# Attention division moved under the tail, output by chunks, shorter roots, one table load and two orders moved, in an eight-stage transformer kernel

## The chip, the core and the metric

The kernel runs on one core of one Trainium2 chip. The core has TensorE (PE in the profile, with PEld for its weight loads), VectorE (DVE), ScalarE (ACT), GpSimd (POOL) and SyncE, whose queue (SPq) issues most transfers. The metric is the device time of one execution in microseconds, lower is better. The time before is the median of three executions, 3603.91 us (3601.78 to 3606.88). The profiled execution took 3613.86 us, with a span of 3612.1 us from its first to its last instruction.

## What is computed

Eight stages follow one another on 4096 tokens of width 128: four times an attention-like layer and a mixture of experts, each behind a layer norm and added to the stream `x`. Only what the change touches is shown.

```python
def _layernorm(x, axis=-1, eps=1e-05):
    m = jnp.mean(x, axis=axis, keepdims=True)
    v = jnp.var(x, axis=axis, keepdims=True)
    return (x - m) / jnp.sqrt(v + eps)
...
# layer 0 and layer 1 attention (16 heads of 8; layer 1 causal)
    probs = jax.nn.softmax(scores, axis=-1)
    a_dot = jnp.einsum('bnst,btnd->bsnd', probs, v4)
...
# layer 0 also reads a memory through elu(q)
    out = (a_dot * (1.0 - w) + a_mem * w).reshape(B, S, D_MODEL)
...
# layer 2 attention: two selective scans, forward and backward
    u = jnp.swapaxes(jax.nn.silu(xc + conv_b[None, :, None]), 1, 2)
...
# layer 3 mixture, the last stage: 16 routed experts and a shared one
    y = jnp.einsum('bsed,bse->bsd', ye, combine).astype(x.dtype)
    x = x + _L3_ffn_ref(_layernorm(x, axis=-1), ...)
```

## The kernel before

`x` and `h` lie in SBUF as [128 features, 4096 tokens] and are worked on in 8 chunks of 512 (`NB`, `chunk(c)`). Each stage is one or more blocks. In a block every engine has its own list of instructions, in the order in which the code writes them, and engines meet through semaphores; a block ends when all its engines are through. No scheduler moves anything: what stands first in the code of an engine is issued first, and an instruction that waits holds up all behind it on that engine.

**Norm.** `layer_norm` (five times), `layer_norm_twice` (once) and the head of `mixture` (four times) take means and variances on TensorE, the square root on ScalarE, and then a chain of small VectorE operations on [128, 32] (a Newton step on the reciprocal root, then a split into three bf16 parts), each waiting for the one before it (`Chain`). TensorE then spreads the root over the chunks.

**First projection.** `layer0_project` runs 8 passes. In pass c ScalarE copies q, k and v out of PSUM with some functions of q, then squares three weight tiles of the next mixture (`sq`, a ring of 3, line 1447), then does `copy_num(c-1)` (line 1411) and `widen(c-1)` (line 1417). TensorE in its pass c does the denominators and numerators of c, the projection of c+2, counts the squares of the pass (`count_squares`, lines 1374 and 1378, forms of one column), and last `spread_inverse(c)` (line 1366), which needs `widen(c)`, that is the end of ScalarE's pass c+1. `sq` of job n needs the count of job n-3.

**Second projection.** `pattention` with `a=a` (names a1q_) does the same for layer 1. SyncE stores for each chunk v, then the three parts of q (ready by VectorE, line 1846), then the three parts of k (ready by GpSimd, line 1694), then issues loads for the attention to come. The chunk buffers are used in turns of two, so ScalarE's copies for chunk c wait for the stores of chunk c-2.

**Attention.** `attend` handles query blocks b of 512 in 8 steps; the products of a block lag half a block behind its scores. The row maxima go out through a small DRAM buffer (line 1040) and come back into the queries (line 1043), both by GpSimd's DMA queue; TensorE's `scores_of_keys` waits for them. Numerators and denominators of each block and group of four heads (`pv_sb`, 256 KB) are stored by SyncE at line 947 in `a.pv`. At the end SyncE waits for all these stores (line 986), and the block ends.

**Division.** `combine` is a block of its own. It loads the 128 rows of denominators (line 1557) and, in four buffers, the numerators of the 8 blocks (line 1561). GpSimd builds 0/1 matrices (`pick`); VectorE inverts the denominators (line 1584); TensorE spreads them over the rows (line 1579); VectorE multiplies (line 1590, or 1592 and 1595 where the result is weighted and added to `x`).

**Scan and end.** In the norm before the scan ScalarE ends with Exp (line 2008), and the scan begins with SiLU (line 2163). The last mixture adds its chunks to `x` (line 715); a block behind it stores `x` in one transfer of 2 MB (line 2968).

## Time and profile before

| | us |
|---|---|
| three executions | 3603.91, 3601.78, 3606.88 |
| the profiled execution | 3613.86 |
| its span | 3612.1 |
| first projection | 32.0 to 137.5 |
| first attention | 137.5 to 552.8 |
| its division | 552.8 to 573.0 |
| first mixture | 573.0 to 1080 |
| second projection | 1104 to 1195.3 |
| second attention | 1195.3 to 1561 |
| its division | 1561 to 1578 |
| rest of layer 1 | 1578 to 1940 |
| scan | 1985.8 to 2940 |
| last mixture | 3180 to 3612.1 |

The mean granted TensorE clock over the span is 0.926 of full speed. The page names the releaser of an idle time behind an arrow: `[1.72 <-ACT ...]` says that the engine was idle for 1.72 us and that ScalarE ended it. In the rows a timeline entry with `x3` is a run of like instructions, whose length is from the start of the first to the end of the last. In the view of stretches the busy times follow in the order PE, PEld, DVE, ACT, POOL, then come the granted clock, the DMA share and GB/s.

### The profile page before, as it was taken

How to read it: one execution, taken by the hardware profiler on the slowest of the kernel's cores; microseconds unless marked ns; L12 is line 12 of the kernel's file. 1: busy time of each engine (PE TensorE's matmuls, PEld its weight loads, DVE VectorE, ACT ScalarE, POOL GpSimd, SP SyncE). 2: the span in 40 equal slices, each digit the busy share in tenths (PEclk: the TensorE clock that was granted, in tenths of full speed). 3: DMA queues.
4: the chain of work that ended last, by engine and by line, in shares of the span. 5: the costliest groups of instructions: out<-in, count | busy, mean ns of one | idle time of the engine just before them, and what ended most of it. 6: DMA issues, size and time to landing. Idle time of an engine off the chain costs nothing. (4 is left out here: it accounts for less than half of the span.)

```text
span 3612.1 us, 39566 instructions
## 1 busy us (share of the span) xinstructions
PE 3240.8 (90%) x12845; PEld 1536.3 (43%) x12845; DVE 2450.0 (68%) x4164; ACT 1820.7 (50%) x2881; POOL 1191.2 (33%) x1010
## 2 busy tenths in 40 slices
PE   8899998999997699979998789898898789889999
PEld 5422224444444354535544233333333354764443
DVE  4788874443338577746544899999999955656544
ACT  5366672444446355534333777777777633312221
POOL 4211110000002222210000799999999910210000
PEclk7699998999998799989899899999999979889999
DMA  4222201000002533110000443443443410000000
GB/s 129 66 69 65 61 31 33 1 0 1 1 19 81 132 88 91 60 39 1 1 1 25 153 153 147 148 157 144 155 152 147 147 45 3 1 1 1 0 1 24
DMA packets 113335, 232.14 MB, mean 64 GB/s; under 512 B 27701, under 2 KB 82378, under 8 KB 95754
## 3 DMA queue, kind: packets, MB, share of 16 engines
q1 hardware_dynamic: 109034, 228.02, 19.0%
q0 software_dynamic: 4096, 1.59, 0.2%
q8 instruction: 104, 1.70, 0.2%
q14 instruction: 101, 0.83, 0.1%
HBM read 191.46 MB, written 34.87 MB: 63 GB/s over the span
## 5 line engine op out<-in xcount | busy, mean ns | idle before, releaser
L1199 DVE TENSOR_REDUCE a_top<-a_sc 128x1 f32<-128x512 f32 (+3 forms) x1024 | 547.2, 584 | 162.3 <-PE a_sc L1075 102.5
L2406 POOL TENSOR_TENSOR a_g<-a_g,a_spread 128x1024 f32<-128x1024 f32 x255 | 597.7, 2363 | 41.4 <-DVE a_g L2336 40.8
L2336 DVE TENSOR_TENSOR_SCAN a_g<-a_decay,a_drive 128x512 f32<-128x512 f32 x510 | 587.1, 1201 | 16.3 <-ACT a_drive L2225 12.9
L1156 ACT ACTIVATE a_prob<-a_st 128x1024 f32<-128x1024 f32 (+2 forms) x512 | 422.5, 862 | 280.7 <-PE a_st L1092 182.9
L705 DVE TENSOR_TENSOR f_s<-f_a,f_spread 128x512 f32<-128x512 f32 x392 | 269.4, 687 | 381.8 <-PE f_y L547 170.6
L2084 PE MATMUL a_y<-a_g,ident 128*128 128x512 f32 x1024 | 481.0, 610 | 31.3 <-POOL a_g L2406 31.3
L538 PE MATMUL f_hid<-h,f_w 128*128 128x512 f32 x784 | 404.2, 597 | 0.0
L547 PE MATMUL f_y<-f_s,f_w 128*128 128x512 f32 x784 | 401.6, 594 | 2.6 <-DVE f_s L705 2.6
L2209 ACT ACTIVATE a_decay<-a_delta,a_capped_a 128x512 f32<-128x512 f32 x512 | 331.8, 710 | 12.4 <-DVE a_g L2336 9.7
L1072 PE MATMUL a_sc<-a_k,a_q 96*128 96x512 bf16 (+3 forms) x1024 | 311.4, 357 | 20.9 <-POOL a_mask_k L996 11.2
L2084 PEld LDWEIGHTS a_y<-a_g,ident 128*128 128x128 f32 x1024 | 198.4, 197 | 306.7 <-issue 246.1
L602 ACT ACTIVATE f_a<-f_hid,f_b,f_norms 128x512 f32<-128x512 f32 x256 | 198.8, 777 | 255.2 <-PE f_hid L538 255.2
L1089 PE MATMUL a_st<-a_q,a_k 128*128 128x512 bf16 (+3 forms) x1024 | 284.0, 346 | 29.9 <-DMA a_q<-a_max_rows 28.2
L1107 PE MATMUL a_pv<-a_prob,a_v 128*32 128x512 f32 (+3 forms) x2048 | 234.7, 527 | 0.6 <-ACT a_prob L1156 0.3
L620 POOL CAST f_gates_f<-f_gates_b 96x512 f32<-96x512 bf16 x24 | 14.7, 612 | 653.6 <-ACT f_gates_b L583 653.6
L547 PEld LDWEIGHTS f_y<-f_s,f_w 128*128 128x128 f32 x784 | 146.4, 189 | 196.4 <-issue 177.5
L2380 POOL TENSOR_TENSOR a_pd<-a_du_s,a_spread 128x1024 f32<-128x1024 f32 x96 | 227.2, 2366 | 0.1
L602 ACT ACTIVATE f_a<-f_hid 128x512 f32<-128x512 f32 x136 | 81.2, 597 | 289.6 <-PE f_hid L535 289.6
L753 DVE TENSOR_TENSOR f_m<-f_a,f_hid 128x512 f32<-128x512 f32 x136 | 93.6, 688 | 181.0 <-ACT f_a L602 180.6
L538 PEld LDWEIGHTS f_hid<-h,f_w 128*128 128x128 f32 x784 | 148.0, 191 | 158.0 <-issue 151.7
L2325 DVE TENSOR_TENSOR a_drive<-a_du,a_spread 128x512 f32<-128x512 f32 x320 | 203.6, 682 | 0.0
L1089 PEld LDWEIGHTS a_st<-a_q,a_k 128*128 128x128 bf16 x1024 | 86.9, 98 | 252.4 <-ACT a_prob L1156 114.6
(396 smaller groups left out, 4903.0 us busy)
## 6 DMA issues: line engine op xcount, KB each, us to landing
a_spread<-a_bc_rows SPq DMA_DIRECT2D x128, 1024.0 KB, 4.6
a_q<-a_q_rows SPq DMA_DIRECT2D x192, 96.0 KB
a_pv_rows<-a_pv_sb SPq DMA_DIRECT2D x48, 256.0 KB, 2.0
a_k<-a_k_rows SPq DMA_DIRECT2D x288, 32.0 KB
a_k<-a_k_rows SPq DMA_DIRECT2D x288, 16.0 KB
a_num<-a_pv_rows SPq DMA_DIRECT2D x16, 256.0 KB, 3.6
a_pv_rows<-a1q_vf SPq DMA_DIRECT2D x16, 256.0 KB, 2.1
a_q_rows<-p_qp SPq DMA_DIRECT2D x24, 128.0 KB
```

What stands on the lines that cost most here:

```text
L538: nc.tensor.matmul(hid[:, n % 4, :], unit.w1, h[:, chunk(c)], start=True, stop=True).then_inc(f.hidden, 1)
L547: nc.tensor.matmul(y[:, :], f.units[u].w2, s[:, (n - LAG) % R, :], start=(u == 0), stop=(u == U - 1 and f.b2 is None)).then_inc(f.used, 1)
L602: nc.scalar.activation(a[:, n % R, :], hid[:, slot, :], f.func, bias=unit.bias if unit.bias is not None else 0.0, scale=unit.scale if unit ...
L705: nc.vector.tensor_tensor(s[:, n % R, :], (m if gated else a)[:, n % R, :], spread[:, k % 2, :], ALU.mult).then_inc(f.scaled, 1)
L1072: last = nc.tensor.matmul(sc[:, at % 3, 0:w], q[k][0:MAX_AT, n, t * P:(t + 1) * P], kk[k][0:MAX_AT, n // HK, 0:w], start=True, stop=not a. ...
L1089: last = nc.tensor.matmul(st[:, j % 2, col:col + wide], kk[k][:, n // HK, key:key + P], q[k][:, n, first:first + wide], start=True, stop=n ...
L1156: nc.scalar.activation(prob[w % 2][:, j, 0:width(kp)], st[:, j % 2, 0:width(kp)], ACT.Exp, scale=a.scale).then_inc(s.exp_done, 1)
L1199: nc.vector.tensor_reduce(top[:, t, n:n + 1], sc[:, slot(4 * n + t) % 3, 0:w], AX.X, ALU.max).then_inc(s.maxed, 1)
L2084: last = nc.tensor.matmul(y[:, k, :], S.ident[:, :], g[:, n % 8, k, :], start=False, stop=(n == STATES - 1))
L2209: last = nc.scalar.activation(decay[:, n % 4, k, :], delta[:, d, k, :], ACT.Exp, scale=capped_a[d][:, k, n:n + 1])
L2336: nc.vector.tensor_tensor_scan(to, decay[:, n % 4, k, way], drive[:, k, way], 0.0, ALU.mult, ALU.add).then_inc(scanned, 1)
L2406: nc.gpsimd.tensor_tensor(g[:, n % 8, :, :], g[:, n % 8, :, :], spread[:, pair % 4, 2 + n % 2:3 + n % 2, :].to_broadcast([P, H2, L]), ALU. ...
```

## The change

Six things are changed. They are shown here cut to their core.

1. **Roots.** In all ten norms the separate addition of EPS goes, and three operations with three operands take the place of four (in `layer_norm_twice`, where the two additions stay, two take the place of three).
2. **Output.** In the last mixture SyncE stores each chunk when it is added; the block behind it is gone.
3. **Table.** ScalarE does a SiLU of one column at the end of the scan's norm.
4. **Division.** Its buffers lie in the query and key buffers of even blocks (`a.q`, `a.k`). When the scores of block 6 are done, SyncE loads the denominators of blocks 0 to 6 (112 rows) and the first four numerators within the attention block, ahead of the last three stores; GpSimd builds the pick matrices and VectorE inverts the 112 rows there. The wait for the last stores moves into the division's block, where the last 16 rows of denominators come as four small transfers and are inverted between chunks 4 and 5.
5. **First projection.** `copy_num(c-1)` and `widen(c-1)` stand ahead of the squares.
6. **Second projection.** The parts of k are stored ahead of those of q.

```diff
-            chain = Chain(dve, S.ln_step, 7 * call)
-            nc.vector.tensor_scalar(v[:, :], var[:, :], EPS, None, ALU.add)
+            chain = Chain(dve, S.ln_step, 6 * call)
             chain(nc.vector.reciprocal(rstd[:, :], std[:, :]))
-            chain(nc.vector.tensor_tensor(v[:, :], v[:, :], rstd[:, :], ALU.mult))
-            chain(nc.vector.tensor_tensor(v[:, :], v[:, :], rstd[:, :], ALU.mult))
-            chain(nc.vector.tensor_scalar(v[:, :], v[:, :], -0.5, 1.5, ALU.mult, ALU.add))
-            chain(nc.vector.tensor_tensor(rstd[:, :], rstd[:, :], v[:, :], ALU.mult))
+            chain(nc.vector.scalar_tensor_tensor(v[:, :], var[:, :], EPS, rstd[:, :], ALU.add, ALU.mult))
+            chain(nc.vector.scalar_tensor_tensor(v[:, :], v[:, :], -0.5, rstd[:, :], ALU.mult, ALU.mult))
+            chain(nc.vector.scalar_tensor_tensor(rstd[:, :], v[:, :], 1.5, rstd[:, :], ALU.add, ALU.mult))
...
-def mixture(nc, S, f):
+def mixture(nc, S, f, out=None):
...
+            if out is not None:
+                for c in range(NB):
+                    sp.wait_ge(f.added, c + 1)
+                    sp.dma_start(out[:, chunk(c)], S.x[:, chunk(c)]).then_inc(S.stored, 16)
+                sp.wait_ge(S.stored, 16 * NB)
...
@@ attend, sync @@
                 body(b, True, True, b % 2)
+            sp.wait_ge(s.st_done, (nB + NB - 1) * 32)
+            for k in range(2):
+                sp.wait_ge(s.pv_stored[k], 16 * 2 * (nB + NB - 1))
+            sp.dma_start(m.den[0:EARLY, :], m.rows[0:EARLY, DH, :]).then_inc(m.den_loaded, 16)
+            for b in range(4):
+                sp.dma_start(m.num[:, b, :], m.rows[H * b:H * b + H, 0:DH, :]).then_inc(m.num_loaded[b], 16)
             body(NB, False, True, 0)
-            for k in range(2):
-                sp.wait_ge(s.pv_stored[k], 16 * 2 * (nB + NB))
+            a.pv_landed = [(s.pv_stored[k], 16 * 2 * (nB + NB)) for k in range(2)]
...
@@ attend, gpsimd and vector @@
+            pool.wait_ge(s.st_done, (nB + NB - 1) * 32)
+            build_picks(nc, pool, m)
...
+            dve.wait_ge(m.den_loaded, 16)
+            nc.vector.reciprocal(m.den[0:EARLY, :], m.den[0:EARLY, :]).then_inc(m.inverse, 1)
...
@@ layer0_project, scalar @@
                 nc.scalar.activation(vf[k][:, :, :], v_ps[:, :, 0:KV], ACT.Copy).then_inc(s.copied, 1)
+                if c >= 1:
+                    copy_num(c - 1)
+                    widen(c - 1)
                 for n in jobs_of(c):
...
-                if c >= 1:
-                    copy_num(c - 1)
-                    widen(c - 1)
...
+EARLY = H * (NB - 1)
+def build_picks(nc, pool, m):
+    nc.gpsimd.memset(m.pick, 0.0).then_inc(m.picked, 1)
+    nc.gpsimd.memset(m.pick_last, 0.0).then_inc(m.picked, 1)
+    nc.gpsimd.memset(m.den_last, 1.0).then_inc(m.picked, 1)
+    pool.wait_ge(m.picked, 3)
...
@@ combine, sync @@
+            for landed, value in a.pv_landed:
+                sp.wait_ge(landed, value)
+            sp.wait_ge(m.picked, 5)
+            for q in range(4):
+                sp.dma_start(m.den_last[32 * q:32 * q + H, :], m.rows[EARLY:EARLY + H, DH, q * P:(q + 1) * P]
+                             ).then_inc(m.last_loaded, 16)
+            for b in range(4, NB):
+                sp.wait_ge(m.multiplied, b - 3)
+                sp.dma_start(m.num[:, b % 4, :], m.rows[H * b:H * b + H, 0:DH, :]).then_inc(m.num_loaded[b % 4], 16)
...
@@ combine, tensor @@
+                if b < NB - 1:
+                    last = nc.tensor.matmul(inv[:, b % 4, :], m.pick[0:EARLY, b, :], m.den[0:EARLY, :],
+                                            start=True, stop=True)
+                else:
+                    pe.wait_ge(m.last_inverse, 1)
+                    for q in range(4):
+                        last = nc.tensor.matmul(inv[:, b % 4, q * P:(q + 1) * P], m.pick_last[:, q, :], m.den_last,
+                                                start=True, stop=True)
...
@@ combine, vector @@
-            dve.wait_ge(den_loaded, 16)
-            nc.vector.reciprocal(den[:, :], den[:, :]).then_inc(inverse, 1)
             for b in range(NB):
+                if b == 5:
+                    dve.wait_ge(m.last_loaded, 64)
+                    nc.vector.reciprocal(m.den_last, m.den_last).then_inc(m.last_inverse, 1)
...
@@ pattention, sync @@
+                    sp.wait_ge(pj.k_parts, pc + c + 3)
+                    store_parts(sp, a.k_rows, c, kp[k], pj.stored[k])
                     sp.wait_ge(pj.q_parts, pc + c + 3)
                     store_parts(sp, a.q_rows, c, qp[k], pj.stored[k])
-                    sp.wait_ge(pj.k_parts, pc + c + 3)
-                    store_parts(sp, a.k_rows, c, kp[k], pj.stored[k])
...
@@ layer2_mamba, Prepare.scalar @@
+                nc.scalar.activation(warm[:, :], S.eps[:, 0:1], ACT.Silu)
```

Three places show how the instructions stand. The first is ScalarE in the first projection, from the copy of k in pass 1 to the copy of q in pass 2. Before:

```order
L1437 ACTIVATE p_k<-p_qk_ps 64x512
L1439 ACTIVATE p_kp<-p_k 64x512
L1441 ACTIVATE p_v<-p_v_ps 128x256
L1447 ACTIVATE p_sq<-f_w 128x512 x3
L1411 ACTIVATE p_num_f<-p_num 128x512
L1417 ACTIVATE p_inv_w<-p_inv_t 128x512
L1424 ACTIVATE p_q<-p_qk_ps 128x512
```

After:

```order
L1446 ACTIVATE p_k<-p_qk_ps 64x512
L1448 ACTIVATE p_kp<-p_k 64x512
L1450 ACTIVATE p_v<-p_v_ps 128x256
L1420 ACTIVATE p_num_f<-p_num 128x512
L1426 ACTIVATE p_inv_w<-p_inv_t 128x512
L1459 ACTIVATE p_sq<-f_w 128x512 x3
L1433 ACTIVATE p_q<-p_qk_ps 128x512
```

The three squares moved behind the copy of the numerators and the widening.

The second is SyncE's queue at the end of the first attention and in its division; the branches are the ends of blocks. Before:

```order
L843 DMA a_q<-a_q_rows 24x4x512
L846 DMA a_k<-a_k_rows 8x2x512 x3
L947 DMA a_pv_rows<-a_pv_sb 128x512 x9
L875 UNCONDITIONAL_BRANCH
L1555 UNCONDITIONAL_BRANCH
L1557 DMA a_den<-a_pv_rows 128x512
L1561 DMA a_num<-a_pv_rows 128x1x512 x8
```

After (the new names `a_q` and `a_k` are the buffers that the denominators and numerators now share with queries and keys):

```order
L842 DMA a_q<-a_q_rows 24x4x512
L845 DMA a_k<-a_k_rows 8x2x512 x3
L947 DMA a_pv_rows<-a_pv_sb 128x512 x6
L987 DMA a_q<-a_pv_rows 112x512
L989 DMA a_q<-a_pv_rows 128x1x512 x4
L947 DMA a_pv_rows<-a_pv_sb 128x512 x3
L875 UNCONDITIONAL_BRANCH
L1591 UNCONDITIONAL_BRANCH
L1597 DMA a_k<-a_pv_rows 16x128 x4
L1601 DMA a_q<-a_pv_rows 128x1x512 x4
```

Five loads moved ahead of the last three stores, and four small ones are new.

The third is ScalarE from the scan's norm into the scan. Before:

```order
L2008 ACT_TABLE_LOAD
L2008 ACTIVATE a_neg_a<-a_pack 128x32 x2
L122 UNCONDITIONAL_BRANCH
L2453 UNCONDITIONAL_BRANCH
L2163 ACT_TABLE_LOAD
L2163 ACTIVATE a_u<-a_bank,a_pack 128x512 x2
```

After:

```order
L2048 ACT_TABLE_LOAD
L2048 ACTIVATE a_neg_a<-a_pack 128x32 x2
L2049 ACT_TABLE_LOAD
L2049 ACTIVATE a_warm<-eps 128x1
L122 UNCONDITIONAL_BRANCH
L2494 UNCONDITIONAL_BRANCH
L2204 ACTIVATE a_u<-a_bank,a_pack 128x512 x2
```

The load of the SiLU table moved from the scan's block into the norm's, with one small operation behind it.

## Rows read from the trace of the kernel before

**Rows 1.** The page, section 1: engine, busy us, share of span, instructions.
```profile
PE 3240.8 (90%) x12845; PEld 1536.3 (43%) x12845; DVE 2450.0 (68%) x4164; ACT 1820.7 (50%) x2881; POOL 1191.2 (33%) x1010
```

**Rows 2.** The timeline at the end (start us, us, engine line op).
```profile
3605.41 0.34 SPq L2968 DMA_DIRECT2D out_xT<-x  x1
```

**Rows 3.** The DMA issues by line: queue, count, KB each, median us to landing.
```profile
a_pv_rows<-a_pv_sb SPq DMA_DIRECT2D x48, 256.0 KB, 2.0
...
out_xT<-x SPq DMA_DIRECT2D x1, 2048.0 KB, 6.3
```

**Rows 4.** The timeline, VectorE, first norm's root, and one three-operand operation.
```profile
23.28 0.19 DVE L193 TENSOR_SCALAR ln_v<-ln_var 128x32 f32<-128x32 f32 x1 [3.99 <-ACT ln_std L232]
...
24.66 0.18 DVE L200 CAST ln_parts<-ln_rstd 128x32 bf16<-128x32 f32 x1
...
1996.98 0.19 DVE L2287 SCALAR_TENSOR_TENSOR a_capped_a<-a_bank,a_neg_a 128x32 f32<-128x32 f32 x1
```

**Rows 5.** The timeline, ScalarE, where the scan begins.
```profile
1985.84 1.28 ACT L2163 ACT_TABLE_LOAD   x1 [14.13 <-PEq L122]
...
1987.14 1.27 ACT L2163 ACTIVATE a_u<-a_bank,a_pack 128x512 f32<-128x512 f32 x2
```

**Rows 6.** The timeline around the end of the first attention and its division.
```profile
534.62 15.57 SPq L947 DMA_DIRECT2D a_pv_rows<-a_pv_sb  x3
...
552.84 0.32 SPq L1557 DMA_DIRECT2D a_den<-a_pv_rows  x1
...
555.58 3.35 DVE L1584 RECIPROCAL a_den<-a_den 128x512 f32<-128x512 f32 x1 [22.56 <-DMA a_den<-a_pv_rows]
...
561.23 0.69 DVE L1592 TENSOR_TENSOR a_num<-a_num,a_inv 128x512 f32<-128x512 f32 x1 [2.30 <-PE a_inv L1579]
...
571.97 0.75 DVE L1595 SCALAR_TENSOR_TENSOR x<-a_num,w_dot,x 128x512 f32<-128x512 f32 x1
```

**Rows 7.** The stretches, same place: PE, PEld, DVE, ACT, POOL busy, then PEclk.
```profile
551.00:552.00 1.00, 0.00 (x0) 0.00 (x0) 0.00 (x0) 0.00 (x0) 0.00 (x0) 1.00 0.42 154
```

**Rows 8.** The timeline at the end of the second attention and its division.
```profile
1558.68 0.32 SPq L947 DMA_DIRECT2D a_pv_rows<-a1q_vf  x1
...
1569.69 0.69 DVE L1590 TENSOR_TENSOR a_g<-a_num,a_inv 128x512 f32<-128x512 f32 x1 [2.30 <-PE a_inv L1579]
...
1577.11 0.69 DVE L1590 TENSOR_TENSOR a_g<-a_num,a_inv 128x512 f32<-128x512 f32 x1 [0.16 <-DMA a_num<-a_pv_rows]
```

**Rows 9.** The DMA issues between 1545 and 1580 us.
```profile
a_num<-a_pv_rows SPq DMA_DIRECT2D x8, 256.0 KB, 3.8
```

**Rows 10.** The timeline, TensorE waiting for a DMA, quiet and beside block loads.
```profile
538.05 0.11 PEld L1089 LDWEIGHTS a_st<-a_q,a_k 128*128 128x128 bf16 x2 [0.88 <-DMA a_q<-a_max_rows]
...
1237.17 0.10 PEld L1089 LDWEIGHTS a_st<-a_q,a_k 128*128 128x128 bf16 x1 [8.35 <-DMA a_q<-a_max_rows]
```

**Rows 11.** The view of line 1043, a_q<-a_max_rows, its last line.
```profile
DMA to landing us min/median/max: 2.0/2.3/6.3
```

**Rows 12.** The timeline, TensorE in the first projection's loop.
```profile
73.69 2.07 PE L1366 MATMUL p_spread<-ident,p_inv_w 128*128 128x128 f32 x8 [1.72 <-ACT p_inv_w L1417]
...
82.39 1.04 PE L1345 MATMUL p_v_ps<-p_wkv,h 128*128 128x64 f32 x8
...
87.83 2.08 PE L1366 MATMUL p_spread<-ident,p_inv_w 128*128 128x128 f32 x8 [1.72 <-ACT p_inv_w L1417]
```

**Rows 13.** The timeline, ScalarE in that loop.
```profile
84.30 0.63 ACT L1447 ACTIVATE p_sq<-f_w 128x512 f32<-128x512 f32 x1 [5.82 <-PE p_sums L1374]
```

**Rows 14.** The stretches in that loop, columns as in rows 7.
```profile
113.00:114.00 1.00, 1.00 (x8) 1.00 (x7) 0.00 (x0) 1.00 (x3) 0.00 (x0) 0.58 0.18 52
```

**Rows 15.** The timeline, SyncE and GpSimd in the second projection.
```profile
1129.00 1.21 POOL L1694 TENSOR_TENSOR a1q_kp<-a1q_k_rest,a1q_kp 128x512 bf16<-128x512 f32 x1
...
1133.13 1.87 SPq L1224 DMA_DIRECT2D a_q_rows<-a1q_qp  x3
```

**Rows 16.** The timeline, ScalarE, last chunk of the second projection.
```profile
1185.57 0.60 ACT L1780 ACTIVATE a1q_qp<-a1q_q_ps 128x512 bf16<-128x512 f32 x1 [2.79 <-DMA a_k_rows<-a1q_kp]
```

115 lines of the change are left out of this document (54 added, 61 removed).

## The prediction

> **What bounds the kernel now.** I read the engine totals first. TensorE is busy for 3240.8 us, 90% of the span [rows 1], so a change pays only where TensorE also stands still, or where a serial tail has no TensorE work in it. I then read the timeline at the joints which the diff touches. At each, the reader should ask which instruction ends last and who is free meanwhile. The profiled execution took 3613.86 us against a median of 3603.91, which is 0.28% more. I work out differences in it and carry them over as they are, since none is a share of the whole.
>
> **Output.** The last instruction of the program is one store of 2 MB [rows 2]; stores of its kind land 6.3 us after issue, one of 256 KB after 2.0 us [rows 3]. By chunks, seven of eight stores lie beside the last chunks' work, and only the last one's landing is left: 6.3 - 2.0 = **-4.3 us**. If the joint with the removed block costs something too, it is a few tenths more. If the stores still queued up, it could not exceed the old landing, so the bounds are 0 and -4.5.
>
> **Roots.** From the first VectorE step of the root to the split into parts, 24.66 - 23.28 = 1.38 us pass, in six waits of one step for the next, some 0.23 us each [rows 4]. A three-operand operation of the same size takes 0.19 us there, as the two-operand one does, so the fused steps are not longer. Of the chain before the split stand the division, a little longer than the rest (0.38), and three steps of 0.225: 1.05 us. That is 0.32 us in nine norms and 0.25 in the tenth: **-3.1 us**. TensorE waits for the root in each, so nothing hides it; the bounds are -2 and -4.
>
> **Table.** When the scan begins ScalarE has been idle for 14.13 us; it loads its table for 1.28 us and starts the SiLU 1.30 us after the load began [rows 5]. The load moves into that idle time: **-1.3 us**. What it costs if the 14.13 us were not there is the same 1.3 us, earlier. The row shows 0.02 us between load and SiLU. The Trainium skill (page "ScalarE: Activation LUTs", section "What ACT_TABLE_LOAD costs") gives about 1283 ns for the load, which the trace agrees with (1.28 us), and about 1380 ns of draining besides, which the trace doesn't show. By that page the term would be -2.7 and the sum 1.4 us lower.
>
> **Division of the first attention.** Its last store is issued by 534.62 + 15.57 = 550.19 us. Then, one after the other, the stores land, the denominators are loaded (issued 552.84), VectorE inverts them from 555.58 for 3.35 us, and the first product starts at 561.23, 2.30 us behind the inverse; the last ends at 572.72 [rows 6]. In the new order the block ends when the last store is issued. With some 0.3 us for the joint, TensorE starts the first spread at 550.5, with its inverse done. It comes straight from work: the stretch behind 551 shows the full clock (1.00) [rows 7]. So I take 1.1 us for the first spread and its wait; the old 2.30 bounds it from above. First product 551.6. The products' chain of 572.72 - 561.23 = 11.49 us stays, 1.44 a block. The second inversion is of 128 columns and adds 3.35 x 128/512 = 0.84, with its wait 0.9. Last product ends at 551.6 + 11.49 + 0.9 = 564.0: -8.7 us. Numerators 4 to 7 must be there: the last stores land by 550.2 + 2.0 = 552.2, four small loads go out by 553.5, numerator 4 follows and lands 3.8 us later [rows 9], at about 557.9, and product 4 is due at 551.6 + 4 x 1.44 = 557.4. So this is just in time; at most 0.5 us is lost.
>
> Against it stands what moves ahead. 1.25 MB of loads are now issued near 535 to 537.5 us, ahead of the last three stores on SyncE's queue, and the last block's queries wait there for their row maxima: TensorE already stood for 0.88 us at 538.05, and where block loads ran beside that round trip it stood for 8.35 us [rows 10]. The landing of that load is 2.0, 2.3 or 6.3 us (minimum, median, maximum) [rows 11]. So the early loads cost from 0 to 6.3 - 2.2 = 4.1 us. No row has five large loads in just this place; I take +1.5, nearer the quiet end, since the denominators' load is spread over 112 rows and the round trip is half over when they go out. Net **-7.2 us** (-4.6 to -8.7).
>
> **Division of the second attention.** Last store issued by 1559.0, first product 1569.69, last ends 1577.80 [rows 8]. New: first product at 1559.0 + 0.35 + 1.1 = 1560.4. Here a block takes only 8.11/8 = 1.01 us, so the transfers come last: stores land 1561.0, four small loads until 1562.2, numerator 4 issued then and landing 0.6 + 3.8 us later at 1566.6, while its product would be due at 1564.5. From there product 4, the second inversion (0.9) and three products of 0.69 end at 1570.2: -7.6. The same contention, with less traffic around, is +0.7 (0 to 4): **-6.9 us**.
>
> **First projection.** TensorE's passes are 87.83 - 73.69 = 14.14 us apart, and each begins with 1.72 us of waiting for the widened inverse of ScalarE, which stands behind the three squares [rows 12]. There are four such waits. The squares themselves wait for the counts (5.82 us) [rows 13], so ScalarE is not the bound but sits in a ring with TensorE: counts at a pass's end let the squares run, these let the widening run. With the widening ahead of the squares, the spread no longer waits for it: 3 x 1.72, and 1.2 for the first, where ScalarE now has to wait some 0.5 us for VectorE's inverse before it gets to its squares: **-6.4 us**. The bounds are 0, if a wait of the counts for the squares takes the old one's place, and more by what a better clock gives (a rival below).
>
> **Second projection.** GpSimd has the parts of k ready at 1129.00 + 1.21 = 1130.2, SyncE issues the store of q's at 1133.13 for 1.87 us [rows 15] and only then k's. The row of k's store first lets its 1.9 us of issuing begin before q's are there. The last chunk's ScalarE copy waits 2.79 us for that buffer's store [rows 16]; of it the PSUM copy's own readiness leaves about 0.8. **-2.0 us** (0 to -2.8). Other chunks don't gain: TensorE sets their pace.
>
> **Sum:** -4.3 - 3.1 - 1.3 - 7.2 - 6.9 - 6.4 - 2.0 = -31.2, so the forecast is 3603.9 - 31.2 = **3572.7 us** (the profiled execution's span would become about 3581). No step is expected to cost time elsewhere: the pick matrices are built by GpSimd in blocks where it has nothing else left.
>
> **Rivals.**
>
> *The clock stays up in the first projection.* Between 73.69 and 82.39 us, 8.7 us, TensorE runs at 1.2 GHz [rows 12], and forms that take half as long at 2.4 GHz could save up to 4.35 us a pass. ScalarE's own work would then bound the pass at about 10.2 instead of 12.4 us, so 2.2 us over four or five passes: 9 to 11 us more, 3562. For it: the waits of 1.72 us, idle time ahead of the slow part, vanish. Against it: the granted clock was at 0.58 between 113 and 114 us with TensorE busy for the whole of that stretch, in the counting of one column a form [rows 14]; it fell without idleness. The Trainium skill (page "TensorE: Matmul & The Clock Gate", section "Part 1: The HAM clock gate") ties the half clock to an idle engine; by that rule this rival would be the forecast; the row speaks against it. Chance 0.13.
>
> *Contention at both tails is large.* Each round trip of the last row maxima takes 6.3 us, not 2.3: 4.1 - 1.5 + 4 - 0.7 = 6 us worse, 3578.5. For it: the 8.35 us wait [rows 10]; against it: the large loads go out while the round trip is partly done. Chance 0.2.
>
> *One large part does not do what it says.* Either the ring of squares holds the passes at 14.14 us, so that the wait turns up ahead of the counts, or an attention's early block end is lost because the last products or copies of the block end later than the last store's issue by some microseconds. Either costs 6 to 7 us; both give 3585. Chance 0.13 that one or both hold.
>
> *Slower.* The buffers of the division are those of the even query blocks. If the layout or the shifted loads disturb the second attention at its block ends, the row maxima of every block could meet block loads as at 1237.17. One such wait costs 8.35 - 0.88 = 7.5 us; seven of them make 52 us, for a total of 3625. It decides from about five such new waits, where the gain of 31 us is used up. Against it: within blocks 0 to 6 the order of SyncE's queue is the same as before, only the tail moves. Chance 0.02.
>
> **How the numbers follow.** The forecast has a chance of 0.52, between 3566 and 3578: its bounds are the single terms' (first spread up to 1.1 us later in either division, contention 2 us either way, projection 3 us). I reach up to 3585 for the two rivals above it and down to 3560 for the clock, which leaves out less than 2 in 10. Faster by over 0.2%, about what a measurement of this kernel can tell from no change, means below 3596.7, and all but the slower rival and a coincidence of failures lie there: 0.94. Within 0.2%: 0.04; slower: 0.02.
>
> **What would show it.** In the changed trace: a last store of 256 KB, landing in about 2 us; some 1.05 us from the root's first step to its split; no table load in the scan's block; a first product within 1.5 us of each attention's last issued store, a small inversion of about 0.85 us, last products near 13 and 11 us behind that store; TensorE's wait for the last row maxima under 3 us (about 6 if the second rival holds); passes of 12.4 us without a wait ahead of the spread (10 with the clock high, 14 if the ring holds); the last chunk's ScalarE wait near 0.8 us. Wrong would be: new waits at the row maxima of earlier blocks, a wait for squares ahead of the counts, or numerators 4 to 7 landing late by more than 2 us.

## The result

The changed kernel took 3559.88 us in the median of four executions (3552.98 to 3563.64), the kernel before, measured beside it, 3605.39 us (3601.78 to 3614.10). The ratio is 0.9868, with a 95% interval of 0.9844 to 0.9892: about 47 us less, where 31 were forecast. The measured median lies 0.12 us below the range's low end of 3560. In a second comparison the changed kernel had 0.9874 (0.9853 to 0.9896).

The two profiled executions differ by more: spans of 3612.1 and 3557.1 us, 55 us. To see where, I use marks that both traces have, and the time between each mark and the next. "Cast" is VectorE's rounding of the row maxima, of which each attention has 32. "First inverse" is VectorE's first reciprocal of the projection's denominators (`p_inv_t`).

| stretch (us) | before | after | difference | forecast |
|---|---|---|---|---|
| first projection, from its first inverse to the first cast | 104.95 | 88.27 | -16.7 | -6.4 |
| first attention, first to last cast | 380.48 | 380.26 | -0.2 | 0 |
| last cast to last product of its division | 40.37 | 31.29 | -9.1 | -7.2 |
| double norm and second projection, to the first cast | 118.12 | 115.37 | -2.8 | -2.3 |
| second attention, first to last cast | 336.27 | 325.36 | -10.9 | 0 |
| last cast to last product of its division | 33.88 | 25.65 | -8.2 | -6.9 |
| start of the last addition to the end of the span | 7.65 | 3.08 | -4.6 | -4.3 |

The engine totals after, beside [rows 1]: TensorE is still busy for 90% of a shorter span.

```profile
PE 3212.4 (90%) x12785; PEld 1527.4 (43%) x12857; DVE 2441.6 (69%) x4147; ACT 1820.5 (51%) x2882; POOL 1193.7 (34%) x1016
```

The end, from the timeline of VectorE and SyncE and the list of transfers after 3540 us, answers to [rows 2, 3]: the last chunk is added at 3554.02, its store is issued 0.02 us after that and lands in 2.0 us.

```profile
3554.02 0.69 DVE L716 TENSOR_TENSOR x<-x,f_y 128x512 f32<-128x512 f32 x1 [1.48 <-PE f_y L548]
...
3554.73 0.33 SPq L459 DMA_DIRECT2D out_xT<-x  x1
```

```profile
out_xT<-x SPq DMA_DIRECT2D x1, 256.0 KB, 2.0
```

The root in the first norm, beside [rows 4]: 24.36 - 23.29 = 1.07 us where it was 1.38, with each fused operation at the 0.19 us of a plain one.

```profile
23.29 0.35 DVE L193 RECIPROCAL ln_rstd<-ln_std 128x32 f32<-128x32 f32 x1 [3.98 <-ACT ln_std L230]
23.68 0.19 DVE L194 SCALAR_TENSOR_TENSOR ln_v<-ln_var,ln_rstd 128x32 f32<-128x32 f32 x1
23.91 0.19 DVE L195 SCALAR_TENSOR_TENSOR ln_v<-ln_v,ln_rstd 128x32 f32<-128x32 f32 x1
24.13 0.19 DVE L196 SCALAR_TENSOR_TENSOR ln_rstd<-ln_v,ln_rstd 128x32 f32<-128x32 f32 x1
24.36 0.18 DVE L198 CAST ln_parts<-ln_rstd 128x32 bf16<-128x32 f32 x1
```

ScalarE at the scan's start, beside [rows 5]: the second table load now stands behind the first one's work, and the SiLU starts without one. What was 15.4 us from the Exp's end to the SiLU is 14.3 us here (12.9 in the second trace of the changed kernel). The 1.4 us between the two traces are the clock's, as far as the rows show: TensorE ends this wait, and its granted clock over the stretch was 0.68 here and 0.76 there (0.70 before).

```profile
1923.38 1.28 ACT L2049 ACT_TABLE_LOAD   x1
1924.67 0.20 ACT L2049 ACTIVATE a_warm<-eps 128x1 f32<-128x1 f32 x1
1937.65 1.26 ACT L2204 ACTIVATE a_u<-a_bank,a_pack 128x512 f32<-128x512 f32 x2 [12.78 <-PEq L122]
```

The first division, beside [rows 6]. These lines are of SyncE and VectorE, in order of time. The early loads go out at 507.64 to 510.78, the inversion of 112 rows (3.33 us) stands inside the attention, the last store is issued by 532.67, the first product starts 1.8 us behind it, and the last ends 13.8 us behind it (22.5 before).

```profile
507.64 0.34 SPq L987 DMA_DIRECT2D a_q<-a_pv_rows  x1
508.03 2.75 SPq L989 DMA_DIRECT2D a_q<-a_pv_rows  x4
...
515.15 0.68 DVE L1196 CAST a_max_row<-a_sc 16x512 bf16<-16x512 f32 x1 [2.52 <-PE a_sc L1127]
515.76 3.33 DVE L1216 RECIPROCAL a_q<-a_q 112x512 f32<-112x512 f32 x1
...
525.97 6.70 SPq L947 DMA_DIRECT2D a_pv_rows<-a_pv_sb  x2
...
534.47 0.69 DVE L1632 TENSOR_TENSOR a_q<-a_q,a_inv 128x512 f32<-128x512 f32 x1 [15.38 <-PE a_inv L1611]
...
541.39 0.95 DVE L1625 RECIPROCAL a_k<-a_k 128x128 f32<-128x128 f32 x1
...
545.69 0.75 DVE L1635 SCALAR_TENSOR_TENSOR x<-a_q,w_dot,x 128x512 f32<-128x512 f32 x1
```

The second division, beside [rows 8], has TensorE's last wait for row maxima in it, too. The first product again starts 1.8 us behind the last store's issue (1518.15), the last ends 10.6 us behind it; product 4 waits 1.90 us for its numerators, as the forecast had it.

```profile
1496.97 0.36 SPq L987 DMA_DIRECT2D a_q<-a_pv_rows  x1
...
1509.24 0.22 PE L1099 MATMUL a_st<-a_mask_k,ident_b 128*128 128x128 bf16 x1 [0.25 <-DMA a_q<-a_max_rows]
...
1517.83 0.32 SPq L947 DMA_DIRECT2D a_pv_rows<-a1q_vf  x1
...
1519.95 0.69 DVE L1630 TENSOR_TENSOR a_g<-a_q,a_inv 128x512 f32<-128x512 f32 x1 [12.92 <-PE a_inv L1611]
...
1525.12 0.69 DVE L1630 TENSOR_TENSOR a_g<-a_q,a_inv 128x512 f32<-128x512 f32 x1 [1.90 <-DMA a_q<-a_pv_rows]
...
1528.05 0.69 DVE L1630 TENSOR_TENSOR a_g<-a_q,a_inv 128x512 f32<-128x512 f32 x1 [0.19 <-PE a_inv L1616]
```

The first projection, TensorE's spreads, beside [rows 12]: no wait ahead of these four (a wait of 1.47 us is ahead of a later one, at 105.98), and they are not evenly apart. From 68.80 to 80.06 it is 11.3 us, from there to 89.37 it is 9.3, then 11.2.

```profile
68.80 2.02 PE L1375 MATMUL p_spread<-ident,p_inv_w 128*128 128x128 f32 x8
...
80.06 1.14 PE L1375 MATMUL p_spread<-ident,p_inv_w 128*128 128x128 f32 x8
...
89.37 2.06 PE L1375 MATMUL p_spread<-ident,p_inv_w 128*128 128x128 f32 x8
...
100.60 1.14 PE L1375 MATMUL p_spread<-ident,p_inv_w 128*128 128x128 f32 x8
```

Its stretches (PE, PEld, DVE, ACT, POOL busy, then the granted clock) show why: in the short pass the clock is at 0.97.

```profile
70.00:80.00 10.00, 10.00 (x50) 7.48 (x49) 5.79 (x8) 6.54 (x13) 3.61 (x3) 0.72 0.37 103
80.00:90.00 10.00, 8.99 (x59) 7.05 (x60) 5.79 (x8) 8.02 (x15) 3.62 (x3) 0.97 0.40 111
90.00:100.00 10.00, 10.00 (x48) 7.54 (x47) 5.79 (x8) 6.60 (x15) 3.61 (x3) 0.69 0.43 119
```

In the last chunk of the second projection ScalarE's copy waits 0.77 us, and for TensorE, where it waited 2.79 us for a store [rows 16].

```profile
1156.08 0.60 ACT L1820 ACTIVATE a1q_qp<-a1q_q_ps 128x512 bf16<-128x512 f32 x1 [0.77 <-PE a1q_q_ps L1757]
```

So two questions stood: why the first projection gave 16.7 us instead of 6.4, and why the second attention, which the change doesn't touch, gave 10.9.

### The profile page after: what moved, and what is told of

Its sections match the earlier page's. It is cut to its first block and busy times, and to the rows that moved or that the text cites. A ratio compares the mean times of both kernels' runs of the same rounds, so it can differ in the third digit from the quotient of the medians.

```text
span 3557.1 us, 39516 instructions
## 1 busy us (share of the span) xinstructions
PE 3212.4 (90%) x12785; PEld 1527.4 (43%) x12857; DVE 2441.6 (69%) x4147; ACT 1820.5 (51%) x2882; POOL 1193.7 (34%) x1016
## 5 line engine op out<-in xcount | busy, mean ns | idle before, releaser
L2250 ACT ACTIVATE a_decay<-a_delta,a_capped_a 128x512 f32<-128x512 f32 x512 | 331.8, 710 | 12.6 <-DVE a_g L2377 9.8
L1096 PE MATMUL a_st<-a_q,a_k 128*128 128x512 bf16 (+1 forms) x952 | 264.4, 341 | 10.1 <-issue 5.9
L752 DVE TENSOR_TENSOR f_m<-f_a,f_hid 128x512 f32<-128x512 f32 x136 | 93.5, 687 | 182.2 <-ACT f_a L603 181.7
```

Of the source, the lines that this page charges most:

```text
L1096: last = nc.tensor.matmul(st[:, j % 2, col:col + wide], kk[k][:, n // HK, key:key + P], q[k][:, n, first:first + wide], start=True, stop=n ...
L2250: last = nc.scalar.activation(decay[:, n % 4, k, :], delta[:, d, k, :], ACT.Exp, scale=capped_a[d][:, k, n:n + 1])
```

## Experiments

### One part alone, and all but one

The kernel before once more gave one execution of 3601.91 us.

> The kernel before once more, for a second trace. In the first pair of traces the second attention (from its first cast of a row maximum to its last) took 336.3 us before and 325.4 us after, 10.9 us less, which my forecast did not have. Theory N (it varies from one execution to the next with the landing of the 12 KB row maxima): here it differs from 336.3 us by several us, and the sum of TensorE's waits for those maxima differs from the 25 us of the first trace. Theory O (the change gives it): 336.3 us again, within 1 us. The first projection should be as it was: the first cast of the first attention at 151.9 us, passes 14.1 us apart, either way.

Its second attention took 328.6 us, 7.6 less than in the first trace, and TensorE's waits for the row maxima summed to 18.0 us instead of 26.0. The first projection repeated, 104.8 us. Theory N has the upper hand over O already: the same kernel varies there.

The new order of ScalarE alone:

```diff
                 nc.scalar.activation(vf[k][:, :, :], v_ps[:, :, 0:KV], ACT.Copy).then_inc(s.copied, 1)
+                if c >= 1:
+                    copy_num(c - 1)
+                    widen(c - 1)
                 for n in jobs_of(c):
...
-                if c >= 1:
-                    copy_num(c - 1)
-                    widen(c - 1)
```

> The kernel before with the order of ScalarE in the first projection alone (inverse widened ahead of the squares). Theory C (the pause of 1.72 us let the clock fall, so without it both the pause and the slow part go): the first cast of the first attention comes at about 151.9 - 16.7 = 135.2 us, passes of 10 to 12 us, and the time falls by 16.7 us, ratio 0.9954. Theory P, my forecast's step (the pause alone goes, the clock falls as before): 151.9 - 6.4 = 145.5 us, ratio 0.9982. Nothing should change in the second attention by either; if it does, it varies by itself.

Ratio 0.9977 (0.9964 to 0.9991), 8.3 us. The projection took 93.5 us in the trace, 11.4 less than before, between the two theories. From the first division to the double norm this trace needs 3.1 us more, 519.9 us where the one before has 516.8. In the head of the first mixture, 29 us slices from the division's end, the granted clock was 0.68 and 0.76 here, 0.74 and 0.89 before. The order isn't shown to cause this: the small parts alone (below), with the old order, have 519.8 us there with the same 0.68 and 0.76, and the order with the join and k's store first has 516.0.

All but that order (the diff above, reversed, on the changed kernel):

> The changed kernel with the old order of ScalarE in the first projection. Theory C: about 16.7 us slower than the changed kernel, so 3561 + 16.7 = 3577 us or 0.992 of before; the cast of the first attention at 151.6 us. Theory P with the remainder from elsewhere: 0.989 (6.4 us slower than the changed kernel only). Second attention: Theory O (the change gives the 10.9 us) says about 325 us from first to last cast here; Theory N says anything from 325 to 337.

Ratio 0.9913 (0.9896 to 0.9929), 31.4 us; the changed kernel's further 14 to 16 us are the order's, with an error of about 10. The projection took 101.2 us, the second attention 330.3.

The join alone. Its edit is item 4 of the change, whole; two places of it:

```diff
+            dve.wait_ge(m.den_loaded, 16)
+            nc.vector.reciprocal(m.den[0:EARLY, :], m.den[0:EARLY, :]).then_inc(m.inverse, 1)
...
-            dve.wait_ge(den_loaded, 16)
-            nc.vector.reciprocal(den[:, :], den[:, :]).then_inc(inverse, 1)
```

> The kernel before with the division's join alone (both attentions). My forecast's terms were 8.7 and 7.6 us with contention at the tails of 1.5 and 0.7 us (net 14.1). Theory J (no contention at all, chains as worked out): from the last cast of a row maximum to the last product 40.37 to 31.3 us in layer 0 and 33.9 to 25.8 us in layer 1, that is 17.2 us less, ratio 0.9952. Theory K (part of what the changed kernel's trace shows at the tails comes from the other parts): less than 15 us. The casts of the first projection should not move by more than the clock there varies.

Ratio 0.9945 (0.9930 to 0.9961), 19.8 us. In the trace the stretches from last cast to last product took 31.6 and 25.7 us: 8.8 and 8.1 us less. Theory J held: there is no contention in the tails.

The stores' order alone (the two lines for q stood ahead of those for k):

```diff
                     sp.wait_ge(pj.k_parts, pc + c + 3)
                     store_parts(sp, a.k_rows, c, kp[k], pj.stored[k])
+                    sp.wait_ge(pj.q_parts, pc + c + 3)
+                    store_parts(sp, a.q_rows, c, qp[k], pj.stored[k])
```

> The kernel before with k's parts stored ahead of q's in the second projection alone. My forecast: 2.0 us from it, ratio 0.9994, which no timing can tell, so the trace is asked: from the root of the double norm to the first cast of the second attention 118.1 us before, 116.1 by my forecast, 115.9 in the changed kernel (which also has the shorter root, 0.25 us). Second attention from first to last cast: Theory O (the order of the stores gives a part of the 10.9 us) says about 325 us here; Theory N (it varies by itself: 336.3, 328.6, 330.9, 336.1, 330.3 us in five traces so far) says anything between 325 and 337.

Ratio 1.0000 (0.9988 to 1.0012), as no timing could tell. The trace has 115.75 us for the double norm and second projection instead of 118.1: 2.4 us. Its second attention, 330.5 us, lies in Theory N's range and not at Theory O's 325.

The small parts alone (items 1 to 3 of the change):

```diff
-            chain(nc.vector.tensor_scalar(v[:, :], v[:, :], -0.5, 1.5, ALU.mult, ALU.add))
-            chain(nc.vector.tensor_tensor(rstd[:, :], rstd[:, :], v[:, :], ALU.mult))
+            chain(nc.vector.scalar_tensor_tensor(v[:, :], v[:, :], -0.5, rstd[:, :], ALU.mult, ALU.mult))
+            chain(nc.vector.scalar_tensor_tensor(rstd[:, :], v[:, :], 1.5, rstd[:, :], ALU.add, ALU.mult))
...
+                nc.scalar.activation(warm[:, :], S.eps[:, 0:1], ACT.Silu)
...
+                for c in range(NB):
+                    sp.wait_ge(f.added, c + 1)
+                    sp.dma_start(out[:, chunk(c)], S.x[:, chunk(c)]).then_inc(S.stored, 16)
```

> The kernel before with the shorter roots, the output by chunks and the early table load alone. My forecast's terms: 3.1 + 4.3 + 1.3 = 8.7 us, ratio 0.9976. In the traces so far the first projection took 104.9 us with the old root and its old order, but 101.2 us with the new root and its old order. Theory F (a shift of 0.2 us of its start moves where the clock falls and rises in it): 101.2 us here too, and 12 us in sum. Theory G (that was one execution's chance): 104.9 us.

Ratio 0.9987 (0.9975 to 0.9998), 4.7 us with 8.7 at the interval's edge. The projection took 101.1 us. That looks like Theory F, but the join alone, with the old root, had 101.7 us as well, so the root is not the reason.

### What lowers the clock in the first projection

In the kernel before, TensorE got idle matmuls ahead of its wait for the widened inverse:

```diff
             def spread_inverse(c):
+                if FILL and 1 <= c < NB - 1:
+                    pe.wait_ge(merged, c)
+                    for t in range(2 * TC):
+                        nc.tensor.matmul(spread[:, (t % TC) * P:(t % TC + 1) * P], S.ident[:, :],
+                                         S.ident[:, :], start=True, stop=True)
                 pe.wait_ge(widened, c + 1)
```

> The kernel before with eight matmuls of 128 columns, whose result nobody reads, put on TensorE ahead of its wait for the widened inverse in passes 1 to 6 of the first projection: work added, no order changed, the pause filled. Theory C (idleness in the pause is what lowers the clock): passes become shorter than 14.1 us although more is done, down to 10 to 12, and the first attention's first cast comes at 135 to 145 instead of 151.9 us. Theory P (the clock falls for another reason): passes stay at 14.1 or grow by up to 0.5 us each, the cast comes at 152 to 155 us. A third way: passes stay at 14.1 with the clock high, if ScalarE's ring with the counts sets them.

More work, less time: the projection took 91.5 us instead of 104.9. The timeline of this kernel's TensorE from 88 us on, and then its stretches; a pass is 99.38 - 89.09 = 10.3 us, at the full clock.

```profile
89.09 2.03 PE L1370 MATMUL p_spread<-ident 128*128 128x128 f32 x16
90.96 1.15 PE L1374 MATMUL p_spread<-ident,p_inv_w 128*128 128x128 f32 x8
...
96.73 2.79 PE L1386 MATMUL p_sums<-ones,p_sq 128*128 128x1 f32 x24
99.38 1.36 PE L1370 MATMUL p_spread<-ident 128*128 128x128 f32 x10
```

```profile
80.00:90.00 10.00, 9.86 (x70) 7.91 (x69) 5.79 (x8) 7.28 (x15) 3.62 (x3) 1.00 0.42 112
90.00:100.00 10.00, 9.86 (x70) 7.91 (x69) 5.79 (x8) 7.55 (x16) 3.61 (x3) 1.00 0.40 107
100.00:110.00 10.00, 9.04 (x74) 8.18 (x72) 7.49 (x10) 7.15 (x13) 3.81 (x3) 1.00 0.32 86
```

The timing does not show these 13 us: the ratio is only 0.9989 (0.9976 to 1.0002), 4.0 us and at most 8.7. In its trace the stretch from the fifth `layer_norm` to the sixth was 155.7 us long instead of 152.5, and the second attention took 336.1 us; but the changed kernel's second trace has 155.1 us in the same stretch, so neither is shown to come from the idle matmuls. Where the rest goes stays open.

The shorter projection speaks for idleness as the cause of the falls, but the idle matmuls also stand right behind the counting. So in the changed kernel they were put elsewhere, between the products for q and for k, where TensorE still waited for 1.01 us:

```diff
                 nc.tensor.matmul(q_ps, w.q[:, :], S.h[:, chunk(c)], start=True, stop=True).then_inc(s.projected, 1)
+                if c >= 3:
+                    pe.wait_ge(merged, c - 2)
+                    for t in range(2 * TC):
+                        nc.tensor.matmul(spread[:, (t % TC) * P:(t % TC + 1) * P], S.ident[:, :],
+                                         S.ident[:, :], start=True, stop=True)
                 pe.wait_ge(s.copied, 3 * c + 2)
```

> The changed kernel with eight matmuls of 128 columns, whose result nobody reads, between the products for q and for k in passes 1 to 5 of the first projection, where TensorE still waited 1.01 us for ScalarE. With filled waits in the kernel before the clock stayed at 1.00 for 40 us and passes took 10.2 us. Theory C: the same here, passes of 9.3 to 10.3 us at full clock, the first attention's first cast at 130 to 134 instead of 134.9 us, so 1 to 4 us faster than the changed kernel. If that wait is not what lowers the clock: passes as in the changed kernel plus up to 1 us each, cast at 135 to 139 us.

The projection took 100.1 us, 11.8 more than in the changed kernel's first trace and more than in any trace of the new order without idle matmuls (below); the ratio is 0.9917 (0.9902 to 0.9933). The stretches of this kernel show a fall with no idle time at all around it, behind the counting that ends at 85:

```profile
84.00:85.00 1.00, 1.00 (x11) 1.00 (x10) 0.00 (x0) 0.63 (x1) 0.00 (x0) 1.00 0.55 124
85.00:86.00 1.00, 1.00 (x10) 1.00 (x10) 0.00 (x0) 0.89 (x2) 0.00 (x0) 0.93 0.40 98
86.00:87.00 1.00, 1.00 (x7) 1.00 (x6) 0.78 (x2) 0.88 (x3) 0.00 (x0) 0.50 0.41 107
```

Then the eight at the first place, but in the changed kernel (the first diff of this part on the changed kernel), and four there in all eight passes (`range(TC)`, no condition on c):

> The changed kernel with the eight idle matmuls of 128 columns ahead of the spread of the inverse, right behind the counting, in passes 1 to 6. The eight between q and k cost 11.8 us: with TensorE busy in every us the clock still fell, right behind the counting. In the kernel before, the eight at this place kept it at 1.00 for 40 us. Theory T (the clock falls behind the thin one-column counting, not in a wait): clock at 1.00 from pass 2 on, passes of 10.3 us (8.3 of work and 2.0 of idle matmuls), first cast at 134 to 138 us, so the same as the changed kernel or up to 3 us slower. Theory C (only the wait matters): the clock falls as in the changed kernel and each of six passes is 1 to 2 us longer, cast at 141 to 147 us.

> The changed kernel with four instead of eight idle matmuls there, in all eight passes. Theory T: if four are enough to keep the clock at 1.00, passes take 9.3 us and the first cast comes at 127 to 132 us, 3 to 8 us ahead of the changed kernel; if not, the clock falls in part of the passes and the cast is at 135 to 142 us. Theory C: 138 to 144 us.

Eight gave a projection of 92.4 us, with the clock at 1.00 from 72 to 96 us, ratio 0.9886 (0.9864 to 0.9909); four gave 98.7 us, ratio 0.9915 (0.9896 to 0.9933), with falls in most passes. The changed kernel in the same comparison had 0.9874. So, with one trace of each, eight idle matmuls right behind the counting held the clock better than eight in the other place, and better than four; but they cost their own 2.0 us a pass, and neither kernel beats the changed one. They also show that it takes no filled pause for this: in the changed kernel there was none in this place, and the clock stayed up for 27 us all the same.

The changed kernel once more:

> The changed kernel once more, for a second trace and a tighter ratio. First ratio 0.9868 (0.9844 to 0.9892), and the two first traces differ by 55 us, of which 10.9 us lie in the second attention, 16.7 us in the first projection and 27.4 us elsewhere. I expect the ratio near 0.987, the first projection (from the root of the first norm's inverse to the first cast) at 88.3 us if its clock repeats for a repeated start, and the second attention from first to last cast between 325 and 331 us.

Median 3557.14 us. Its projection took 96.9 us, not 88.3: it does not repeat. In this trace the passes are the 12 us of my forecast (69.09, 81.70, 93.57, 105.89), TensorE busy throughout and the clock at 0.57, 0.66 and 0.62:

```profile
70.00:80.00 10.00, 10.00 (x37) 6.90 (x36) 5.79 (x8) 5.58 (x11) 3.61 (x3) 0.57 0.36 100
80.00:90.00 10.00, 10.00 (x45) 7.30 (x44) 5.79 (x8) 7.57 (x14) 2.71 (x3) 0.66 0.33 92
90.00:100.00 10.00, 10.00 (x49) 8.45 (x49) 4.06 (x7) 7.36 (x14) 1.89 (x2) 0.62 0.29 85
```

The view of stretches over the whole projection, from the first inverse to the first cast, shows what goes with its length. The lines are of the kernel before, the join alone (below 102 us although its order is the old one), the changed kernel's second trace and its first:

```profile
46.92:151.87 104.95, 91.99 (x378) 63.68 (x376) 65.53 (x94) 46.59 (x87) 26.87 (x31) 0.63 0.33 84
```

```profile
45.77:147.46 101.69, 88.73 (x378) 62.05 (x376) 63.43 (x94) 46.59 (x87) 27.42 (x31) 0.67 0.34 87
```

```profile
46.60:143.45 96.85, 89.87 (x378) 61.59 (x376) 61.27 (x93) 47.59 (x88) 27.59 (x31) 0.64 0.35 91
```

```profile
46.62:134.89 88.27, 79.13 (x378) 52.85 (x376) 60.40 (x93) 47.25 (x88) 27.46 (x31) 0.75 0.38 100
```

Within one order the stage is the shorter, the higher its mean granted clock: 0.63 in the five traces of the old order that took 104.8 to 105.0 us, 0.67 in the three of 101.1 to 101.7; with the new order 0.64, 0.66, 0.68, 0.71, 0.75 and 0.75 for 96.9, 93.5, 93.3, 89.7, 88.3 and 88.3 us. And the new order at 0.64 is still 4.8 us shorter than the old one at 0.67. So about 5 us are the pauses' own (an estimate from these two lines), and the rest of the gain is the clock's. Why the clock falls at other places each time stays open.

### The two stages that vary

Four small loads more in each old division, into a tile nobody reads, to see whether the transfers before it change the second attention:

```diff
             sp.dma_start(den[:, :], rows[:, DH, :]).then_inc(den_loaded, 16)
+            for q in range(4):
+                sp.dma_start(spare[:, q, :], rows[0:H, DH, q * P:(q + 1) * P]).then_inc(spared, 16)
...
+            sp.wait_ge(spared, 64)
```

> The kernel before with four small loads more in each division, into a tile nobody reads. In ten traces the second step of the second attention (from its second to its third cast) took 16.4 to 20.5 us in the six kernels with the old division and 12.1 to 15.7 us in the four with the new one. Theory Q (the number of transfers that SyncE's queue has had before decides how its later ones fall beside the row maxima): below 16 us here. Theory N (chance, or something else of the join): 16 to 21 us.

The second step took 11.8 us and the whole second attention 322.1 us, the shortest with an old division. That fitted Theory Q. The next four kernels combine the parts shown above in other ways:

> The kernel before with the new order of the first projection, the join and k's store first, without the small parts (roots, output, table). First projection with the new order: 88.3, 93.5, 96.9 us in three traces. Theory V (the clock falls in some passes and not in others, whatever the rest of the kernel): again between 88 and 97. Forecast's step as it stood: 98.5. Division: 31.3 and 25.7 us from last cast to last product. Second attention between 325 and 331 us if the join is what keeps it short. Ratio by the sum of the parts: 0.9868 plus 8.7 us of small parts, 0.989.

> The kernel before with the new order of the first projection and the small parts, without the join and with q's store first. Theory V: first projection between 88 and 97 us. If the parts only add: 0.9977 x 0.9987 = 0.9964; if the new order and the new root together let the clock stay up more often than either alone (the changed kernel's two traces: 88.3 and 96.9, the order alone: 93.5), nearer 0.993. Second attention between 328 and 340 us if the old division is what lets it be long.

> The kernel before with the join and k's store first, old order in the first projection: first projection 101 to 105 us, divisions 31.3 and 25.7 us, from the double norm's root to the first cast of the second attention 115.8 us, second attention 325 to 331 us if the join keeps it short, beyond 332 if that was chance.

> The kernel before with the new order of the first projection and four small loads more in each old division. First projection 88 to 97 us by Theory V. Second step of the second attention: Theory Q says below 16 us (11.8 in e_extra_dma), Theory N says anything from 12 to 21.

| | ratio (95%) or one time | first projection | second step | second attention |
|---|---|---|---|---|
| order, join, k first | 0.9895 (0.9876 to 0.9914) | 88.3 | 12.9 | 319.3 |
| order, small parts | 0.9956 (0.9939 to 0.9974) | 89.7 | 20.9 | 333.5 |
| join, k first | 3585.34 us | 104.9 | 16.6 | 327.2 |
| order, loads more | 3598.53 us | 93.3 | 16.4 | 332.8 |

With the loads again the second step was 16.4 us, not below 16: Theory Q fell, by little. Taken together, and without the kernels with idle matmuls:

- First projection with the old order: 101.1 to 105.0 us in eight traces, mean 103.6. With the new order: 88.3, 88.3, 89.7, 93.3, 93.5 and 96.9 us, mean 91.7. The order gives 12 us on average, between 4 and 17 in any one pair. The timings agree within their errors of 5 to 10 us: 8.3 us for the order alone, 11 on top of the small parts, 14 to 16 on top of all else, 18 on top of the join and k's store.
- Second attention (here those with idle matmuls count too): with the old division 322.1 to 339.4 us, mean 332.2, in nine traces; with the new one 319.3 to 330.3 us, mean 326.7, in nine. The means differ by 5.6 us, with standard deviations of 5.1 and 3.2 us, so this is hardly chance, yet the ranges overlap and no run shows a mechanism. Nor is it sure that it belongs to the division: eight of the nine traces with the new one also store k's parts first, and grouped by that store order the means are 327.1 and 331.8 us, nearly as far apart. The two traces that tell them apart have 326.4 us (new division, q first) and 330.5 us (old division, k first), which is less than one kernel varies by itself. What varies can be seen: TensorE's wait in the third group. These are TensorE's lines from the small parts alone (339.4 us) and then from order, join and k first (319.3 us), each the two longest waits of its start.

```profile
1217.07 0.31 PE L1091 MATMUL a_st<-a_mask_k,ident_b 128*128 128x128 bf16 x1 [5.97 <-DMA a_q<-a_max_rows]
1237.41 0.31 PE L1091 MATMUL a_st<-a_mask_k,ident_b 128*128 128x128 bf16 x1 [8.89 <-DMA a_q<-a_max_rows]
```

```profile
1189.89 0.31 PE L1100 MATMUL a_st<-a_mask_k,ident_b 128*128 128x128 bf16 x1 [5.24 <-DMA a_q<-a_max_rows]
1204.11 0.22 PE L1100 MATMUL a_st<-a_mask_k,ident_b 128*128 128x128 bf16 x1 [2.79 <-DMA a_q<-a_max_rows]
```

In both, SyncE issues block loads until 7 us before the second wait's end (1230.5) or beyond it (1205.3); the first wait is nearly the same, the second 6.1 us shorter. Why the new division or k's store should help there stays open.

## Why the prediction was wrong

The direction and every part's sign were right; two terms of the sum were too small and one effect, of which no cause is shown, was not in it. With the sizes that the runs showed, the sum is: 31.2 forecast, 5.6 more for the projection (12 instead of 6.4), 3.2 more for the divisions, some 0.7 for the store order and the output, and 5.6 from the second attention, 46 us. The two timed ratios say 45 to 48.

**First projection, the term that was mis-sized.** The step "With the widening ahead of the squares, the spread no longer waits for it: 3 x 1.72, and 1.2 for the first" priced the waits alone at -6.4 and let the clock fall as before; that it stays up was a rival with a chance of 0.13. The pause ahead of the four spreads did go, in all six traces with the new order (in two of them a wait of 1.47 us came up at a later spread), and at a like clock that was worth about 5 us. What failed is that the clock was left out: its mean over the stage, 0.63 or 0.67 with the old order, was between 0.64 and 0.75 with the new one (0.70 on average, from 0.65), and the order gave 12 us. The clock neither fell as before nor stayed up: it stayed up in none to two of the passes and fell in the others, differently from trace to trace of the same kernel. Three of the six traces gave 15 to 17 us off the 104.9, as my rival had it (though the pass at full clock took 9.3 us and not its 10.2), one gave 8.1 us with passes of 12 us, near the forecast, and two lay between. I had treated as two cases what is a mixture, and the range should have been laid around its mean. The row I put against the rival [rows 14] was right in itself: the clock falls behind the one-column counting with TensorE fully busy, as the kernel with idle matmuls between q and k showed again. But that it falls so in one pass did not mean that it does in each. The Trainium skill (page "TensorE: Matmul & The Clock Gate", section "Part 1: The HAM clock gate") ties the half clock to idleness. That the mean clock rose when the pauses went agrees with it; the falls at full occupancy have no place in it, and the filled pause decides nothing, since the same eight matmuls held the clock where there was no pause.

**Divisions.** The chains came out as worked out: last store to last product 13.8 us in the first (forecast 13.8) and 10.6 in the second (forecast 11.2), first product 1.8 us behind the store's issue in both (forecast 1.4). What failed is the step "1.25 MB of loads are now issued near 535 to 537.5 us". They are issued when the scores of block 6 are done, and this is 7.5 us ahead of the last cast, when the last round trip has not begun: 507.64 with the cast at 515.15, so near 525 in the old trace's time. In the second attention they go out at 1496.97, 6.1 us ahead of its last cast. TensorE's matmuls do not wait at all for the last row maxima in the first attention, and 0.25 us in the second. The contention of 1.5 and 0.7 us, and the rival built on it, did not come. The 0.88 us that I took for TensorE standing at 538.05 [rows 10] belong to a weight load: the matmuls of the kernel before have no wait there, and the changed kernel shows the same 0.88 us for its weight load.

```profile
520.84 0.11 PEld L1096 LDWEIGHTS a_st<-a_q,a_k 128*128 128x128 bf16 x2 [0.88 <-DMA a_q<-a_max_rows]
```

I had read the new loads' place from SyncE's order, which tells what they stand behind, and not from the semaphore that they wait for.

**Second attention.** The forecast had 0 for it, and took one trace's waits as fixed. The kernel before varies there by itself (336.3 and 328.6 us in two traces); the changed kernel's first trace was at the short end and the first trace of before at the long one, so much of the 10.9 us between those two is their luck. A mean difference of 5.6 us remains, whose cause is open, and which the new division and k's store share between them in a way that the runs can't tell. Had my range been widened by that stage's spread alone, it would have held the result.

**The rest** held: output -4.6 (forecast -4.3), root -0.31 per norm (-0.32), second projection -2.4 alone (-2.0), with the last chunk's wait at 0.77 us (0.8), table -1.1 and -2.5 in two traces (-1.3), where what goes beyond the load is the clock's and the shorter root's: load and SiLU stood 0.02 us apart before. That the small parts alone were timed at 4.7 us instead of 8.7 lies within their interval. The rival on the slower side, new waits for row maxima in every block, did not show: the waits of TensorE's matmuls for row maxima in the second attention sum to 17 to 26 us in the traces with the new division, against 18 to 35 with the old.

## What to carry to other kernels

Before a wait is priced, look at the granted clock around it in more than one trace: four pauses of 1.7 us were worth 12 us on average, since the clock moved with them, and by different amounts each time. For work that is moved ahead, place it by the semaphore that it waits for, not by its neighbours in the queue. Look whether a wait is the matmuls' or only a weight load's. And take from one profile only what repeats: two traces of the kernel before would have shown that its second attention goes 8 us either way.

## What the hardware showed beyond that

TensorE's clock fell from 2.4 to 1.2 GHz with the engine busy in every microsecond, behind 24 records of one-column forms (the stretches 84 to 87 above). In the kernel before, eight matmuls of 128 columns that do nothing, 2.0 us of them in each of six passes, went with a projection 13 us shorter where they stood behind those forms; in the changed kernel, standing some 5 us later, they went with one 8 us longer than its order's mean (one trace each). A round trip of 12 KB over GpSimd's queue beside SyncE's block loads cost TensorE 2.8 us in the trace of one kernel and 8.9 in that of another, at the same place of the second attention.
